# Blocks innermost: one contiguous maximum per chunk, and matmuls that step through it

## The reference

```
h = relu(layernorm(x))
XB = h @ B.T
x = x + tanh([h, t] @ W1 + b1) @ W2 + b2 + adj @ XB - rowsum(adj) * XB
h = relu(layernorm(x))
feats = h @ W                                  # 8 heads of 8
scores[head,i,j] = leaky_relu(a_self[i] + a_neigh[j]) - 1e10 * (1 - adj[i,j])
x = x + relu(softmax_j(scores) @ feats + bias)
```

## Time and profile before

| | |
|---|---|
| median of 2 runs | 905.05 us (904.72 to 905.37) |
| the profiled execution | 904.73 us |
| its span, first to last instruction | 903.5 us |
| mean granted TensorE clock | 0.941 |
| PE busy | 776.9 us |
| VectorE busy | 729.3 us |
| ScalarE, GpSimd busy | 128.5, 173.4 us |
| transfers | 281.58 MB, 312 GB/s on average |

### The profile page before, as it was taken

The page is one execution under the profiler, slowest core; times in us unless marked ns, Lnnn a source line. Parts: engine busy times, 40 slices in busy tenths (PEclk is TensorE's granted clock), DMA queues, the critical chain, the costliest instruction groups (busy, mean ns, idle before and its releaser), DMA issues.

```text
span 903.5 us, 13331 instructions
## 1 busy us (share of the span) xinstructions
PE 776.9 (86%) x5222; PEld 266.7 (30%) x5222; DVE 729.3 (81%) x958; ACT 128.5 (14%) x212; POOL 173.4 (19%) x160
## 2 busy tenths in 40 slices
PE   3898999999999999999999999999999999940000
PEld 1333232333333333333332323233333333320000
DVE  5889968989898989898989898998989897952111
ACT  2424011111111111111010201111111111110000
POOL 1000302020110202020202020202011020217774
PEclk9999999999999999999999999999999999985555
DMA  9797879697979797979798897979797979502221
GB/s 375 280 428 288 321 291 422 271 424 288 425 288 426 284 429 280 429 291 418 319 390 364 345 410 300 420 290 422 289 421 287 425 283 429 214 11 40 60 49 41
DMA packets 37267, 281.58 MB, mean 312 GB/s; under 512 B 14336, under 2 KB 18560, under 8 KB 20736
## 3 DMA queue, kind: packets, MB, share of 16 engines
q1 hardware_dynamic: 33152, 277.12, 74.9%
q0 software_dynamic: 4096, 4.20, 2.0%
HBM read 277.10 MB, written 4.19 MB: 311 GB/s over the span
## 4 chain that ended last, share of the span: by engine, by line
PE 74%; POOL 7%; DVE 5%; issue 4%; DMA 4%; SPq 4%; ACT 0%; POOLq 0%; DVEq 0%
PE acc L726 44%; PE row_sums L734 22%; POOL gathered L367 7%; DMA ring<-in_adj_t 4%; SPq L255 4%; DVE max_hi L514 2%; PE ps_hid L754 2%; PE ps_feat L796 1%; PE ps_xb L775 1%; PE ps_acc L768 1%; PE ps_turn L782 1%; PE ps_acc L771 1%; PE ps_acc L773 1%; PE ps_turn L789 1%; DVE max_lo L513 0%
## 5 line engine op out<-in xcount | busy, mean ns | idle before, releaser
L726 PE MATMUL acc<-ring,x_pb 128*64 128x512 f32 x2048 | 462.8, 601 | 18.4 <-DMA ring<-in_adj_t 18.4
L513 DVE TENSOR_TENSOR max_lo<-max_lo,ring 128x2048 f32<-128x2048 f32 x96 | 220.6, 2298 | 44.7 <-DMA ring<-in_adj_t 44.2
L734 PE MATMUL row_sums<-ring,ones_cols 128*32 128x512 f32 x2048 | 240.0, 597 | 0.0
L726 PEld LDWEIGHTS acc<-ring,x_pb 128*64 128x64 f32 x2048 | 141.0, 138 | 326.1 <-issue 326.1
L514 DVE TENSOR_TENSOR max_hi<-max_hi,ring 128x2048 f32<-128x2048 f32 x96 | 219.7, 2289 | 0.0
L358 POOL DMA_INDIRECT cand<-in_adj,cls_row x64 | 78.0, 1218 | 663.5 <-DVE cls_row L543 648.9
L734 PEld LDWEIGHTS row_sums<-ring,ones_cols 128*32 128x32 f32 x2048 | 56.5, 109 | 151.6 <-issue 149.8
L367 POOL DMA_INDIRECT gathered<-feats_dram,best x64 | 62.8, 981 | 19.5 <-issue 19.5
L651 DVE TENSOR_TENSOR gathered<-gathered,bias_row 128x512 f32<-128x512 f32 x8 | 5.6, 703 | 67.5 <-DMA gathered<-feats_dram,best 67.5
L508 DVE TENSOR_TENSOR max_lo<-ring 128x2048 f32<-128x2048 f32 x16 | 36.7, 2292 | 4.4 <-DMA ring<-in_adj_t 2.5
L510 DVE TENSOR_TENSOR max_hi<-ring 128x2048 f32<-128x2048 f32 x16 | 36.6, 2288 | 4.2 <-DMA ring<-in_adj_t 3.9
(11 more groups left out here) (95 smaller groups left out, 423.3 us busy)
## 6 DMA issues: line engine op xcount, KB each, us to landing
ring<-in_adj_t SPq DMA_DIRECT2D x128, 2048.0 KB, 11.3
x_tq<-in_x SPq DMA_DIRECT2D x1, 2048.0 KB, 30.8
feats_dram<-feats SPq DMA_DIRECT2D x16, 128.0 KB, 2.3
out<-gathered SPq DMA_DIRECT2D x8, 256.0 KB
x_pb<-in_x SPq DMA_DIRECT2D x1, 1536.0 KB, 7.8
cand<-in_adj,cls_row POOLq DMA_INDIRECT x64
gathered<-feats_dram,best POOLq DMA_INDIRECT x64
x_pb<-in_x SPq DMA_DIRECT2D x1, 512.0 KB, 4.6
```

Source lines behind the costliest of these rows:

```text
L513: dve.tensor_tensor(max_lo[:, :], max_lo[:, :], lo, ALU.max).then_inc(lo_done, 1)
L726: last = pe.matmul(acc[parity][at:at + D, :], x_pb[:, c * CB + b, :], slot(c)[:, b * W:(b + 1) * W], start=(c == 0 and b < 2), stop=(c == ...
L734: last = pe.matmul(row_sums[at:at + QUAD, :], ones_cols[:, :], slot(c)[:, b * W:(b + 1) * W], start=(c == 0 and b < 4), stop=(c == NC - 1 ...
```

## The change

A chunk becomes 16 blocks of 256 rows in place of 8 blocks of 512. Chunk c holds the blocks of group c // 2 (16 blocks) and the half c % 2 of the strip's rows. Within a partition the 16 blocks of one row are now adjacent, so the chunk is [128, 256 rows, 16 blocks] with the blocks innermost; the host's transposition of `adj_t` is changed to match, and a chunk is still 16 KB per partition in one piece.

- VectorE takes one `tensor_reduce` (maximum over the 16 adjacent blocks, 4096 elements in, 256 out) per chunk, into `part` [128, 4, 512]. `fold_maxima` is left with two steps, 1024 and 512 wide. `max_lo`, `max_hi`, `lo_done`, `hi_done` go; `part`, `part_done` come.
- PE's `products` and `sums` have 16 matmuls each per chunk, 256 columns wide, into one half of `acc` and `row_sums`. Their moving operand is `slot(c)[:, :, b]`: consecutive columns are 16 elements, 64 bytes, apart. `start` stays with the first matmuls of chunk 0, `stop` with the last of chunk 7.
- In the opening PE waits for `pro_norm` of both groups whose blocks a chunk holds: 2, 2, 4, 4, 6, 6, 8, 8 in place of 1 to 8.
- `load` waits for `part_done` where it waited for `hi_done`. The general path uses `part` as its buffer.

```diff
@@ -37,7 +37,9 @@
 CB = 8
 NC = NB // CB
 RING = 4
-HALF = CB * W // 2
+HW = W // 2
+UB = 2 * CB
+NU = NC // 2
 QUAD = 32
 FA = D + 2 * HEADS
 EPS = 1e-5
@@ -227,7 +227,10 @@
                      ps_acc[0:D, :, :]]
         def slot(n):
-            return ring[:, (n % RING) * CB * W:(n % RING + 1) * CB * W]
+            return ring[:, (n % RING) * CB * W:(n % RING + 1) * CB * W].rearrange("p (i b) -> p i b", b=UB)
+
+        def half(c):
+            return slice((c % 2) * HW, (c % 2 + 1) * HW)
         def wide(a, k, n=D):
@@ -262,10 +265,10 @@
             def load(s, c):
                 sp.wait_ge(pe_chunk, s * NC + (c - RING + 1))
-                sp.wait_ge(hi_done, s * NC + (c - RING + 1))
+                sp.wait_ge(part_done, s * NC + (c - RING + 1))
                 sp.sem_inc(sp_past, 1)
                 src = adj_t[bass.ds(s * NC + c, 1)].rearrange("a p f -> (a p) f")
-                sp.dma_start(slot(c), src).then_inc(chunk_in[c % RING], 16)
+                sp.dma_start(slot(c).rearrange("p i b -> p (i b)"), src).then_inc(chunk_in[c % RING], 16)
             def store_feats(s):
@@ -501,28 +504,15 @@
             def fold_chunk(s, c):
-                n = s * NC + c
                 dve.wait_ge(chunk_in[c % RING], s * (16 * NC // RING) + 16 * (c // RING + 1))
-                lo, hi = slot(c)[:, 0:HALF], slot(c)[:, HALF:2 * HALF]
-                if c == 0:
-                    dve.tensor_tensor(max_lo[:, :], lo, hi, ALU.max).then_inc(hi_done, 1)
-                elif c == 1:
-                    dve.tensor_tensor(max_hi[:, :], lo, hi, ALU.max).then_inc(hi_done, 1)
-                else:
-                    dve.wait_ge(hi_done, n)
-                    dve.tensor_tensor(max_lo[:, :], max_lo[:, :], lo, ALU.max).then_inc(lo_done, 1)
-                    dve.tensor_tensor(max_hi[:, :], max_hi[:, :], hi, ALU.max).then_inc(hi_done, 1)
+                dve.tensor_reduce(part[:, c // 2, half(c)], slot(c), AX.X, ALU.max).then_inc(part_done, 1)
             def fold_maxima(s):
-                dve.wait_ge(hi_done, s * NC + NC)
-                dve.wait_ge(lo_done, s * (NC - 2) + NC - 2)
-                dve.tensor_tensor(max_lo[:, :], max_lo[:, :], max_hi[:, :], ALU.max).then_inc(fold, 1)
-                dve.wait_ge(fold, s * 2 + 1)
-                dve.tensor_tensor(max_lo[:, 0:2 * W], max_lo[:, 0:2 * W], max_lo[:, 2 * W:4 * W], ALU.max)\
-                    .then_inc(fold, 1)
-                dve.wait_ge(fold, s * 2 + 2)
-                dve.tensor_tensor(runmax[:, :], max_lo[:, 0:W], max_lo[:, W:2 * W], ALU.max)\
+                dve.wait_ge(part_done, s * NC + NC)
+                dve.tensor_tensor(part[:, 0:2, :], part[:, 0:2, :], part[:, 2:4, :], ALU.max).then_inc(fold, 1)
+                dve.wait_ge(fold, s + 1)
+                dve.tensor_tensor(runmax[:, :], part[:, 0, :], part[:, 1, :], ALU.max)\
                     .then_inc(runmax_done, 1)
             def search_classes(s):
@@ -721,18 +711,18 @@
                 pe.wait_ge(chunk_in[c % RING], s * (16 * NC // RING) + 16 * (c // RING + 1))
-                for b in range(CB):
+                for b in range(UB):
                     at = (b % 2) * D
-                    last = pe.matmul(acc[parity][at:at + D, :], x_pb[:, c * CB + b, :], slot(c)[:, b * W:(b + 1) * W],
-                                     start=(c == 0 and b < 2), stop=(c == NC - 1 and b >= CB - 2))
+                    last = pe.matmul(acc[parity][at:at + D, half(c)], x_pb[:, (c // 2) * UB + b, :], slot(c)[:, :, b],
+                                     start=(c == 0 and b < 2), stop=(c == NC - 1 and b >= UB - 2), skip_group_check=True)
                 return last
             def sums(c):
-                for b in range(CB):
+                for b in range(UB):
                     at = (b % 4) * QUAD
-                    last = pe.matmul(row_sums[at:at + QUAD, :], ones_cols[:, :], slot(c)[:, b * W:(b + 1) * W],
-                                     start=(c == 0 and b < 4), stop=(c == NC - 1 and b >= CB - 4))
+                    last = pe.matmul(row_sums[at:at + QUAD, half(c)], ones_cols[:, :], slot(c)[:, :, b],
+                                     start=(c == 0 and b < 4), stop=(c == NC - 1 and b >= UB - 4), skip_group_check=True)
                 return last
             def chunk(s, c, parity, first=False):
@@ -811,7 +801,7 @@
                         mlp_hidden(s)
             for c in range(NC):
-                pe.wait_ge(pro_norm, c + 1)
+                pe.wait_ge(pro_norm, 2 * (c // 2) + 2)
                 chunk(0, c, 0, first=True)
                 if c == 0:
                     pe.wait_ge(pool_const, 12)
@@ -883,7 +872,7 @@
     w1 = np.asarray(L0_gnn_W1)
     w_gat = np.asarray(L1_gnn_W)
-    tiles = adj.reshape(S, P, TB, P, NC, CB).transpose(0, 4, 3, 5, 2, 1)
+    tiles = adj.reshape(S, P, 2, TB // 2, P, NU, UB).transpose(0, 5, 2, 4, 3, 1, 6)
     arrays = {
         "x": x,
         "adj": adj,
```

More of the change, by code:

```diff
@@ L76, in build @@
         feats = sb("feats", [P, NB * FA])
-        max_lo = sb("max_lo", [P, HALF])
-        max_hi = sb("max_hi", [P, HALF])
+        part = sb("part", [P, NU, W])
         cand = sb("cand", [P, TB, NB])
@@ L154, in build @@
         pe_chunk = sem("pe_chunk")
-        lo_done = sem("lo_done")
-        hi_done = sem("hi_done")
+        part_done = sem("part_done")
         fold = sem("fold")
@@ L243, in _ @@
             for n in range(RING):
-                sp.dma_start(slot(n), adj_t[n]).then_inc(chunk_in[n % RING], 16)
+                sp.dma_start(slot(n).rearrange("p i b -> p (i b)"), adj_t[n]).then_inc(chunk_in[n % RING], 16)
             sp.dma_start(x_tq[:, :, :].rearrange("q (s k) d -> q s (k d)", k=TB), x_by_q).then_inc(x_tq_in, 16)
@@ L691, in _ @@
                             dve.wait_ge(gen_p_turned, n * (NB // 4) + g + 1)
-                            dve.tensor_copy(max_lo[:, (g % 2) * W:(g % 2 + 1) * W], acc[g % 2][:, :])\
+                            dve.tensor_copy(part[:, g % 2, :], acc[g % 2][:, :])\
                                 .then_inc(gen_p_copied, 1)
@@ L868, in _ @@
                                 j = g * 4 + k
-                                at = (g % 2) * W + k * P
-                                last = pe.matmul(ps_hid[:, 0:HD], max_lo[:, at:at + P],
+                                last = pe.matmul(ps_hid[:, 0:HD], part[:, g % 2, k * P:(k + 1) * P],
                                                  feats[:, bass.ds(h * HD + j * FA, HD)],
```

## The result

The changed kernel takes 1616.7 us (median of 2 runs, 1614.67 to 1618.74), where 1595 was forecast. The ratio to the kernel before is 1.787, 95% interval 1.783 to 1.791. The profiled execution took 1618.74 us.

The account below looks back on a forecast made before the run. PE was taken to bound the fifteen strips behind the first. 904.7 + 690 (stepped read) + 5 - 4 (opening) - 1.3 (end) = 1594, say 1595 us; own range 1540 to 1660, 8 in 10 range 900 to 1660.

Parts of the forecast that it names:

- PE sets the time: Fifteen strips behind the first: PE is the bound, busy 47.52 of 47.52 us in a strip, VectorE 43.33.
- The 64-byte step: PE's products and sums: reading every 16th word slows each column, 690 us more over the whole kernel.
- the two prices: PE's stepped read: column time exactly doubled, 660 us more, or 0.92 ns added as in ScalarE's write, 723 us.
- A word from a new place: PE's stepped read: such a word costs about two turns, as for ScalarE, so PE has no spare turn.
- the free step: Rival on PE's stepped read: column time stays 0.84 ns, 910 us in all; chance 0.25.
- the one stream: Rival: only products or only sums pay for the stepped read, 1345 or 1125 us; chance 0.10.
- the queueing streams: Rival: memory serves reads of neighbouring words one after another, 2010 us, or 3910 at ScalarE's price; chance 0.14.
- Count and width: PE's products and sums: 16 matmuls of 256 columns for 8 of 512 cost nothing, 5.16 us a chunk again.
- VectorE: Maxima: eight reductions of 4.40 us, 35.2 us a strip against 34.4 removed; VectorE has room for that.
- The opening: First strip: PE's waits for normalised groups cost 5 us; slow reads make a low clock cheap, 4 us back.
- the walk: First strip at the present matmul rate, followed through VectorE's queue chunk by chunk: the strip ends 6.6 us later.
- The end: After the last chunk: a shorter fold delivers runmax sooner, 1.3 us gained; the gather behind is untouched.

Follow-up runs that it names:

- the four steps: Changed kernel with only the step of PE's reads altered: 1 word 983.08 us, 2 words 1011.87, 4 words 1632.79, 15 words 1591.24.
- the two single streams: Changed kernel, PE's strips unrolled, 16-word step kept in one stream, the other contiguous: step in products alone 1363.69 us, in sums alone 1150.55.
- written out: Changed kernel with PE reading 256 contiguous columns and its fifteen strips unrolled in place of looped: 919.89 us, ratio 1.0165.
- pairs of words at a step of 32: Changed kernel with two neighbouring rows kept adjacent in the layout, nothing left out: 1052.47 us with PE's loop, 993.06 without it.
- 2,576: Kernel before the change, with PE's loop body holding four strips in place of two: 926.24 us, ratio 1.0232.
- the contiguous variant: Changed kernel with products and sums reading 256 contiguous columns in place of every 16th word, PE's loop kept: 983.08 us, ratio 1.089.
- the 256-word run: Changed kernel with blocks outermost: PE reads contiguously, its strips unrolled, VectorE reduces at a step of 256 words: 1224.26 us, ratio 1.353.

## Why the prediction was right, and where it was not

- **PE sets the time.** Right: in the strips of the changed kernel PE never waits for VectorE. Before it did so only twice, 2.2 us in all for h.
- **The 64-byte step, 690 us.** Right in mechanism and nearly in size. In the account above, fifteen strips cost 669 us more (668.0 and the 1.34 of the end), where the same term put 647 there (15 x 8 x 5.39). That is most of the 24 us by which the forecast was low; no errors cancelled. It is 0.91 ns added per column-step (0.90 without the 6.2 us of pauses), at the upper of the two prices, the one from ScalarE's write. At a step of 15 words PE pays exactly double, the lower price; it is the longer beats that bring 16 words up to 0.91, and their cause is open. So that ScalarE's figure fits this well is in part luck. The taking over of a write's price to a read was only argued in the prediction; the four steps and the two single streams show that the read pays, and not why it pays as a write on another engine does. "A word from a new place" was too broad: at a step of 2 words every word is from a new place, and it costs 5%. Of the rivals, the free step, the one stream and the queueing streams all fell.
- **Count and width at nothing.** This step failed, though it cost the forecast almost nothing. The argument looked at the pace of issue and not at the length of the loop body: 24 steps a chunk where 12 stood make a body of 2,312 records that is fetched again in each pass. With the slow read 6.2 us of pauses show; with a fast read it is 63 us. The count and the width themselves are right at nothing: written out, the strips take 3.2 us more in all. "The step is free" was therefore not 910 us, as this rival said, but near 983, and would have been slower by over 2%: the chance of 0.25 for no change hung on a case that this layout and loop could not give.
- **VectorE.** 4.40 us forecast, 4.419 measured, covered in each strip.
- **The opening.** Forecast 8 x 5.39 + 5 - 4 = 44.1 us later, measured 45.9. The slow products of chunks 0 and 4 before (6.19 and 5.25 us where 3.65 is the rate) are the 4 us that came back; for chunk 0 the granted clock reads 1.00, so why it was slow is not shown. The three waits of 3.0 us are there (3.01, 3.01, 3.00). For a fast PE the walk gave 6.6 us; it was 11.6, since the walk gave all matmuls their full rate, and those behind each wait ran at a low granted clock.
- **The end.** The wait of 1.34 us for runmax is gone. PE now waits 0.58 for row_sb, and what is late next had not been asked; but from the last turn to the end of the span it is 106.7 us as against 106.8, so this is made up behind it and the 1.3 us stand.

## What to carry to other kernels

Price an access pattern by how many successive words of a line it takes, on the engine that is the bound: moving the step from the slack engine to the one with no slack costs its whole stream, and a small step can be nearly free: 2 words cost PE 5% and VectorE nothing, pairs of words at a step of 32 cost PE 12%. When an edit turns N instructions into 2N inside a hardware loop, count the records of the loop body, and look behind the branch for idle time put down to issue. A cost measured as zero under a slow engine is not zero: it returns when that engine is made fast.

## What the runs showed that I had not expected

- PE's moving read at one word per 16 bytes costs nearly the same at 4, 15 and 16 words, 14.1 to 14.7 us for 64 records, and two words per 16 bytes 7.5 (step 2) or 8.0 (pairs at 32 words), against 7.13.
- With fast reads a loop body of 2,312 or 2,576 PE records pauses twice at each branch back, 1 to 5 us each. In the contiguous variant half as much again is lost in slow matmuls behind (41 us idle of 63). A body of 1,288 does not pause.
- VectorE's reduction costs 4417 ns at a step of 2 words, 7267 at 256. The Trainium skill, Vector Engine (DVE) Microarchitecture Reference, section 5.2, asks for pairs of adjacent words for the full rate and gives about 1.75 ns for a hop at every element: the 256-word run agrees (7267 ns over 4096 elements, 1.77 ns each), the step of two words does not, and the measurement decides.
- A mean granted clock of 0.76 costs stepped matmuls nothing, and 0.57 costs contiguous ones 70%.
